# Four-layer kernel on 32 batches: layer 1's wide groups alternate between two PSUM banks

## What is computed

```python
def reference(x, t, itok, bias, dt, gate, mask, ...):
    # layer 0: conditioned block; LN is over the whole 256 x 256, scale and shift come from t
    h = silu(scale * LN(x) + shift) @ W_in + b_in
    x = silu(scale * LN(h) + shift) @ W_out + b_out + x
    # layer 1: attention, 16 heads of 16, bias 256 x 256 per head, keys masked by length
    x = LN(x) * (1 + s) + sh
    x = x + softmax(q k^T / 4 + bias, masked) v @ Wo + bo
    x = x + gelu_sigmoid((LN(x) * g2 + beta2) @ W1 + b1) @ W2 + b2      # 256 -> 1024 -> 256
    # layer 2: first and second differences of A*x and B*x on the 256 x 256 grid
    x = maximum(x + dt * df, 0)
    # layer 3: causal attention, then the same wide form with exact gelu, mixed by a gate
    y = x + softmax(causal(q k^T / 4)) v @ Wo + bo
    y = y + gelu(LN(y) @ W1 + b1) @ W2 + b2
    return x + gate * (y - x)
```

## Time and profile before

| | |
|---|---|
| three runs | 2603.47, 2604.91, 2608.86 us |
| median | 2604.91 us |
| the profiled execution | 2604.97 us, of which the span is 2603.7 us |
| TensorE busy | 2470.5 us (95%), 19148 matmuls |
| ScalarE busy | 2115.3 us (81%) |
| VectorE busy | 2043.6 us (78%) |
| GpSimd busy | 1536.1 us (59%) |
| mean granted TensorE clock | 0.984 of full |
| the two wide layers, groups (L1447, TN) | 3072 matmuls, 378.8 us busy, 38.7 us idle before them |

### The profile page before, as it was taken

How to read it: one execution, slowest core, us unless ns; L and a number is a source line. 1 busy time by engine, 2 the same in 40 slices (tenths; PEclk the granted TensorE clock), 3 DMA queues, 4 the chain that set the end, 5 groups by cost and what they waited for, 6 DMA issues and landing times.

```text
span 2603.7 us, 57961 instructions
## 1 busy us (share of the span) xinstructions
PE 2470.5 (95%) x19148; PEld 2005.6 (77%) x19148; DVE 2043.6 (78%) x7387; ACT 2115.3 (81%) x4694; POOL 1536.1 (59%) x1487
## 2 busy tenths in 40 slices
PE   6878999999999999999999999999999999999987
PEld 5666778778877877887887788778878877877776
DVE  6787878788888778888787888878888888878653
ACT  2466888888898888889888888988888888888875
POOL 2566666556666656666665656666556576655421
PEclk6899999999999999999999999999999999999999
DMA  5433443333344333334443333444433344433211
GB/s 205 120 119 105 121 127 113 111 106 106 107 122 126 112 110 108 107 105 122 126 115 108 108 107 106 122 127 115 114 110 100 105 121 125 123 105 96 75 29 33
DMA packets 178537, 287.67 MB, mean 110 GB/s; under 512 B 46080, under 2 KB 99328, under 8 KB 177984
## 3 DMA queue, kind: packets, MB, share of 16 engines
q1 hardware_dynamic: 178240, 283.97, 38.5%
HBM read 174.64 MB, written 8.45 MB: 70 GB/s over the span
## 4 chain that ended last, share of the span: by engine, by line
PE 69%; DVE 15%; SPq 4%; ACT 4%; issue 3%; POOL 2%; DMA 2%; DVEq 0%; POOLq 0%; ACTq 0%
PE bank L1525 17%; PE bank L1447 12%; PE bank L1548 10%; PE bank L1538 6%; PE bank L1563 6%; PE bank L1507 6%; DVE PB L1010 4%; PE bank L1514 3%; SPq L496 3%; PE bank L1459 3%; PE bank L1701 2%; DVE bank L969 2%; PE bank L1436 2%; SPq L492 1%; DMA Ks<-KU 1%
## 5 line engine op out<-in xcount | busy, mean ns | idle before, releaser
L1249 ACT ACTIVATE PB<-PB,mx 128x256 f32<-128x256 f32 (+1 forms) x2048 | 831.4, 473 | 35.7 <-DVE mx L1010 34.7
L579 POOL TENSOR_TENSOR BT<-BT,MN 128x1024 f32<-128x1024 f32 x256 | 556.9, 2180 | 122.5 <-DMA BT<-in_bias 121.0
L1548 PE MATMUL bank<-ident,PB 128*128 128x128 f32 x3584 | 486.4, 274 | 11.5 <-ACT PT L1254 5.5
L1010 DVE CUSTOM_DVE_ANT_0 PB<-bank,BT 128x256 f32<-128x256 f32 x1024 | 372.0, 418 | 137.8 <-PE bank L1538 132.8
L1548 PEld LDWEIGHTS bank<-ident,PB 128*128 128x128 f32 x3584 | 421.6, 141 | 63.4 <-ACT PB L1249 10.6
L1447 PE MATMUL bank<-TN,WS_w 128*128 128x256 f16 x3072 | 378.8, 273 | 38.7 <-ACT BB L1275 19.6
L1538 PE MATMUL bank<-Ks,Qs 96*128 96x512 f32 (+1 forms) x1024 | 364.6, 430 | 25.5 <-DMA Ks<-KU 12.0
L1017 DVE COPY PT<-bank 128x512 f32<-128x512 f32 (+1 forms) x512 | 315.9, 617 | 87.5 <-PE bank L1548 85.8
L1447 PEld LDWEIGHTS bank<-TN,WS_w 128*128 128x128 f16 x3072 | 282.5, 98 | 120.1 <-ACT BB L1275 35.4
L1254 ACT ACTIVATE PT<-bank 128x512 f32<-128x512 f32 (+1 forms) x512 | 272.3, 532 | 94.9 <-PE bank L1548 90.6
L1010 DVE CUSTOM_DVE_ANT_0 PB<-bank,caus 128x128 f32<-128x128 f32 (+1 forms) x1024 | 306.6, 350 | 42.3 <-PE bank L1538 42.2
(11 more groups left out here) (285 smaller groups left out, 4735.9 us busy)
## 6 DMA issues: line engine op xcount, KB each, us to landing
BT<-in_bias SPq DMA_DIRECT2D x256, 512.0 KB, 4.3
Qs<-QH SPq DMA_DIRECT2D x512, 64.0 KB, 2.4
Ks<-KH SPq DMA_DIRECT2D x1024, 32.0 KB, 2.0
Qs<-QU SPq DMA_DIRECT2D x256, 64.0 KB, 2.4
Ks<-KU SPq DMA_DIRECT2D x512, 32.0 KB, 2.0
XT<-in_xT SPq DMA_DIRECT2D x32, 256.0 KB, 2.8
X<-in_x SPq DMA_DIRECT2D x32, 256.0 KB, 2.9
AB<-ada_rows SPq DMA_DIRECT2D x32, 256.0 KB, 3.7
```

The source lines that it names most:

```text
L579: G.op.tensor_tensor(v2(BT[k % 4]), v2(BT[k % 4]), MN[:, :].unsqueeze(1).broadcast_to([128, 2, 512]), ALU.add).then_inc(g_bt, 1)
L1010: V.op.tensor_tensor_reduce(PB[(2 * D + q) % 6][:, h * 256:h * 256 + w], bS[q][:, h * w:h * w + w], plus, -1.0, 3.0e38, ALU.add, ALU.min, ...
L1249: S.op.activation(o, o, ACT.Exp, scale=-1.0, bias=mx[u.layer][:, c:c + 1]).then_inc(a_exp, 1)
L1548: last = T.op.transpose(bP[h][:, c * 128:c * 128 + 128], PB[(2 * u.D + q) % 6][:, h * 256 + k * 128:h * 256 + k * 128 + 128], ident[:, :])
```

## The change

Five things, in one edit.

1. `wide_bank`: for layer 1 in batches 2 to 29 odd groups go to bank 2, even ones stay in bank 1. Group g then waits for the evacuation of group g-2, and for what bank 2 held before: the last output of an earlier batch (`v_o`) and the keys of the next batch (`a_k1`).
2. `key_bank`: layer 1's keys of batches from 3 on go to bank 2. They no longer wait for the queries' evacuation, but for bank 2's readers; the values wait for the queries' evacuation and no longer for the keys'.
3. `t3`, which also uses bank 2, waits in addition for all of layer 1's wide evacuations of the next batch.
4. `P`, `OWN` and `SPLIT` get new ticks; most pieces move a little.
5. `WARM` loses `n1_ones_0`, `win_1`, `w1_0` (three products behind each of four groups), `n2_ones_2`, `n1_ones_3` and `v1_3`; `v3` goes from 10 to 15. In matmuls of the trace: 160 to 120.

```diff
@@ P (and so for OWN and SPLIT)
-    "t1_out": -24, "t1_lo": -21, "x1_bo": -18, "q1": -19, "q1_out": -17, "q1_lo": -27, "k1": -15,
...
+    "t1_out": -24, "t1_lo": -22, "x1_bo": 8, "q1": -18, "q1_out": -18, "q1_lo": -37, "k1": -14,
...
 WARM = {
-    "start": 24, "c1": 12, "n1_ones_0": 2, "v1": 9, "win_1": 5, "w1_0": 3, "n2_ones_2": 1, "n1_ones_3": 4,
-    "v1_3": 1, "v3": 10,
+    "start": 24, "c1": 12, "v1": 9, "v3": 15,
 }
...
+        def key_bank(layer, b):
+
+            return bT_ if layer == 1 and b > 2 else front_bank(layer, b)
...
             if b == NB - 1:
                 return ((bM, bF) if layer == 1 else (bF, bM))[g % 2]
-            return bM if layer == 1 else bT_
+            if layer == 1:
+                return (bM, bT_)[g % 2] if 1 < b < NB - 2 else bM
+            return bT_
...
-                        to_cols(U, front_bank(x, b), a, lambda m: scale_of("p3", 4) if x == 3 and n == "q" else 1.0,
+                        to_cols(U, key_bank(x, b) if n == "k" else front_bank(x, b), a, lambda m: scale_of("p3", 4) if x == 3 and n == "q" else 1.0,
...
                 for b in at(t, f"k{x}"):
-                    T.wait_ge(a_q[x], 3 * b + 2)
-                    linear(front_bank(x, b), "k", H).then_inc(p_k[x], 1)
+                    if x == 1 and b > 2:
+                        T.wait_ge(v_ws, made("w3") + 21)
+                        T.wait_ge(v_o, 2 * (b - 3))
+                        T.wait_ge(v_v[3], b - 2)
+                    else:
+                        T.wait_ge(a_q[x], 3 * b + 2)
+                    linear(key_bank(x, b), "k", H).then_inc(p_k[x], 1)
                     keep(f"k{x}", b)
                 for b in at(t, f"v{x}"):
-                    T.wait_ge(a_k[x], 3 * b + 2)
+                    T.wait_ge(a_q[x], 3 * b + 2)
+                    if x == 3 or b < 3:
+                        T.wait_ge(a_k[x], 3 * b + 2)
...
                 for b, g in steps(t, "w1", 4, 2):
                     T.wait_ge(v_ws, made("p3"))
                     T.wait_ge(v_t2, b + 1)
-                    if b < NB - 1 or g == 0:
+                    if b < 2 or b == NB - 2 or g == 0:
                         T.wait_ge(a_w1, 8 * b + 2 * g)
                     else:
-                        T.wait_ge(v_v[1], NB)
                         T.wait_ge(a_w1, 8 * b + 2 * g - 2)
+                        if b < NB - 1:
+                            T.wait_ge(v_ws, made("w3") + 21)
+                            T.wait_ge(v_o, 2 * (b - 2))
+                            T.wait_ge(a_k[1], 3 * (b + 2) - 1)
+                        else:
+                            T.wait_ge(v_v[1], NB)
...
                     T.wait_ge(v_ws, made("w3") + 21)
+                    if b > 0:
+                        T.wait_ge(a_w1, 8 * min(b + 2, NB - 2))
                     turn(front_bank(3, b), Y3[b % 2]).then_inc(p_t3, 1)
```

More of the change, by code:

```diff
@@ L56 @@
 P = {
-    "score0": -1, "score1": -1, "bias0": 0, "bias1": 0, "exp0": 1, "exp1": 2, "flip0": 8, "flip1": 8, "ev0": 7,
-    "ev1": 9, "pv": 14, "cx": 13, "ct": 17, "pvn": 17, "ld_bt": -12, "mask_add": -23, "stack": -8, "ld_x": -78,
-    "ld_xn": -37, "ld_ab": -36, "ld_mask": -117, "mask": -34, "n1_stats": -75, "n1_ones": -69, "n1_sum": -69,
[6 rows of a table removed]
-    "f1": 74, "s_pm": 63, "s_b": 67, "s_r": 75, "s_rp": 82, "s_re": 96, "s_ha": 81, "s_w": 97, "s_ab": 97,
-    "s_row": 98, "s_mm": 103, "s_f": 103, "ld_w1": -24, "ld_sten": -46, "ld_w3": -277, "coefs": -21,
+    "score0": -1, "score1": -1, "bias0": 0, "bias1": 0, "exp0": 2, "exp1": 2, "flip0": 8, "flip1": 8, "ev0": 7,
+    "ev1": 8, "pv": 14, "cx": 13, "ct": 16, "pvn": 16, "ld_bt": -12, "mask_add": -27, "stack": -8, "ld_x": -97,
+    "ld_xn": -37, "ld_ab": -51, "ld_mask": -96, "mask": -48, "n1_stats": -82, "n1_ones": -68, "n1_sum": -67,
[6 rows of a table added]
+    "f1": 72, "s_pm": 57, "s_b": 71, "s_r": 72, "s_rp": 82, "s_re": 96, "s_ha": 74, "s_w": 97, "s_ab": 97,
+    "s_row": 95, "s_mm": 102, "s_f": 101, "ld_w1": -24, "ld_sten": -46, "ld_w3": -277, "coefs": -21,
     "split_p1": -55, "split_p1_hi": -50, "split_p1_lo": -45, "split_w1": -8, "split_w1_hi": -4, "split_w1_lo": -2,
     "split_p3": 46, "split_p3_hi": 50, "split_p3_lo": 54, "split_w3": 82, "split_w3_hi": 88, "split_w3_lo": 92,
[4 rows of a table removed]
-    "out": 74, "st_out": 71,
[4 rows of a table added]
+    "out": 73, "st_out": 67,
 }
@@ L91 @@
     -2: {
[15 rows of a table removed]
[L107 to L108 removed]
[13 rows of a table added]
+        "m4_b": 325, "ld_x": -111, "ld_xn": -61, "ld_ab": -84, "ld_mask": -20, "ld_bt_1": -17, "stack_1": -10,
+        "s_row": 98, "stack_3": -55, "st_out": 787,
     },
     -1: {
[6 rows of a table removed]
[L117 removed]
[7 rows of a table removed]
[L125 to L127 removed]
[10 rows of a table removed]
[L138 removed]
[8 rows of a table removed]
[L147 to L148 removed]
[7 rows of a table removed]
[L156 removed]
[7 rows of a table removed]
[L164 removed]
[14 rows of a table added]
+        "y3": 489, "m4_rstd": 528, "m4_b": 628, "ld_mask": -163, "ld_x": -110, "ld_xn": -93, "ld_ab": -74,
+        "ld_bt_1": -20, "stack_1": -20, "s_row": 96, "stack_3": -46, "st_out": 990,
+    },
[10 rows of a table added]
+        "pvn_1": 21, "m1": 50, "t2_lo": 50, "f1": 76, "s_r": 79, "s_rp": 87, "s_re": 87, "s_w": 102, "s_ab": 102,
[7 rows of a table added]
+        "m4_b": 47, "scr": -333, "ld_mask": -276, "ld_sten": -223, "ld_ab": -156, "ld_w1": -211, "ld_w3": -39,
+        "ld_bt_1": 3, "stack_1": 5, "s_row": 109, "stack_3": -3, "st_out": 80,
+    },
[15 rows of a table added]
+        "ld_mask": -19, "ld_ab": -35, "ld_bt_1": -1, "stack_1": 2, "s_row": 104, "stack_3": -15, "st_out": 71,
     },
@@ L168 @@
 SPLIT = {
-    "bias1_3": 1, "exp0_3": 2, "exp1_3": 3, "ev0_3": 8, "ev1_3": 10, "pv_3": 13, "cx_3": 12, "ct_3": 16,
-    "pvn_3": 18, "stack_3": -9,
+    "exp0_3": 1, "exp1_3": 3, "flip0_3": 7, "ev0_3": 8, "ev1_3": 9, "ct_3": 17, "pvn_3": 17, "stack_3": -16,
 }
```

9 lines of the change are left out of this document (removed), and 135 rows, old and new, of tables (OWN, P).

## The result

The changed kernel is slower by a little: 2610.89 us (median of 20 runs, 2605.94 to 2615.95) against 2605.12 us for before (20 runs, 2600.05 to 2612.08). The ratio is 1.0019, 95% interval 1.0011 to 1.0027. The prediction was 2595, faster. The time lies inside the range of 2582 to 2612 and on the wrong side of no change.

The account below looks back on a forecast made before the run. TensorE's column work plus its waits was taken to bound the kernel. From 2604.97 us, 7.3 came off for 28 batches at -0.26 and 2.5 for idle-time products, clock and edges 0: 2595 us, range 2582 to 2612.

Parts of the forecast that it names:

- What bounds the kernel, and the steady part: From 500 to 2241 us: TensorE's column work plus its waits set the end; the change gives -0.26 us a batch.
- the waits between the groups: Layer 1's wide groups: alternating banks remove waits for the previous group's evacuation, -0.80 us a batch.
- The wait on TN: t2's new place: the first wide group waits for the turned t2 through ScalarE and VectorE, +0.60 us a batch.
- Layer 3's transposes: Layer 3's wide layer: the ET pair moved ahead covers the eight transposes' wait on the turned t4, -0.23 us a batch.
- The wait on BB: Layer 3's second wide group: its wait for BB's evacuation grows by the moved ET pair, +0.22 us a batch.
- t3's +0.07: Turning Y in bank 2: t3 now waits for all four evacuations, +0.07 us a batch, between 0 and 0.15.
- the keys' term: Layer 1's keys in bank 2: values no longer wait for the keys' evacuation, -0.12 us a batch.
- rival (a): Steady stretch: new tables also remove waits before scores and transposes, 0.42 us a batch, 12 us less, 2583; chance 0.16.
- Idle-time products: Trace matmuls from 160 to 120, mainly at 18.40, 169.45 and 202.64 us: -2.5 us together, between 0 and -3.5.
- Head and last batches: Outside the steady stretch, where tables change by up to a hundred ticks: taken as 0, 6 us allowed either way.
- (b): Steady part: waits only move, 0.26 us a batch more at neighbours cancels the gain, 2602.5 us; chance 0.24.
- (c): t3 stuck behind a late fourth evacuation on ScalarE: 1.0 us a batch lost, slower, 2621 us; chance 0.20.

Follow-up runs that it names:

- e9: The kernel of e7 with layer 1's keys back in bank 0 and the values again behind the keys' evacuation; 2606.70 us, ratio 1.0005.
- e1: The kernel before with the changed kernel's list of idle-time products and nothing else of the change; 2603.76 us, ratio 0.9995.
- e7: The changed kernel with two ticks of the first batch as before, s_pm 56 to 60 and s_re 87 to 97; 2605.99 us, ratio 1.0003.
- e2: The kernel before without the idle-time products w1_0 between the first batch's wide groups; 2603.45 us, ratio 0.9993.
- e11: The kernel before with two first-batch ticks as in the changed kernel, s_pm 60 to 56 and s_re 97 to 87; 2606.82 us, ratio 1.0007.
- e3: The changed kernel with the idle-time products w1_0 put back; 2614.66 us, ratio 1.0027.
- e4: The changed kernel with the whole old list of idle-time products; 2613.74 us, ratio 1.0032.
- e10: The kernel of e8 with layer 3's 43 ticks of the last batch as before the change; 2624.14 us, ratio 1.0067.
- e12: The kernel of e8 with some of GpSimd's ticks of batches 1 and 2 as before; 2606.76 us, ratio 1.0006.
- e13: The changed kernel with s_re alone back at 97 in the first batch; 2611.05 us, ratio 1.0012.
- e14: The changed kernel with s_pm alone back at 60 in the first batch; 2611.66 us, ratio 1.0013.
- e5: The change's two-bank code with the tables and idle-time products of before, but for five ticks that t3 needs; 2672.40 us, ratio 1.0261.
- e6: The changed kernel with its new tables, but the banks and their waits as before; 2681.45 us, ratio 1.0294.
- e8: The kernel of e7 with the first wide group two ticks later in batches 2 to 29, behind P·V; 2605.03 us, ratio 1.0000.

## Why the prediction was wrong

*What bounds the kernel, and the steady part*: right. The period was to fall to 75.4 or 75.5 and is 75.39. By its terms: the waits between the groups, -0.80, are gone whole, 7.25 - 6.38 = 0.87 by the starts. The wait on TN, +0.60, is 0.41 by the idle and 0.62 by the starts (2.07 less 1.45). Layer 3's transposes give the -0.23, but the ET pair moved behind them takes 0.11 more, so -0.12. The wait on BB, +0.22, is (18.7 - 13.7) / 23 = +0.22. t3's +0.07 is 0.72 - 0.66 = +0.06. The ET pair ahead of the values takes 0.22 us (1939.20 to 1939.42) instead of 0.34, the -0.12 of the keys' term, but it takes 0.22 in e9 too, with the keys back in bank 0: the size is right, and the order gives it, not the bank. That makes -0.21. A further -0.18 is the small waits of scores and transposes that are gone, which I had given to rival (a) and counted as 0. Together that is -0.39, and the starts of the batches give -0.35 for the forecast's -0.26: 8.0 us in 23 batches.

*Idle-time products*, -2.5 between 0 and -3.5: not decided. e1 gives a ratio of 0.9995, -1.3 us, with an interval that holds 0 and -2.5. My list of places also left out ten products at 81.7 us and two at 266.7, which have no term in the sum.

*Head and last batches*, 0 with plus or minus 6: **this is the step that failed.** The head measured +12.1, and the last batches +2.5, which the spread of executions covers. I had counted idle time that the new tables could give or take as a share of the idle of before, a sixth of 36.1 us, without following the order of GpSimd and VectorE in any of these batches. The order of the two engines at one place, which was there to be read, held 3.9 us of wait. e7 gives 4.9 us of time back by the medians (2605.99 against 2610.89) and some 4 by the ratios (1.0003 against 1.0019). The other 7 us or so of the head is not settled. At least 3 us of it lie between the first wide groups of batch 1 and batch 3: they are 140.9 to 143.0 us apart in the kernel before, e1, e2 and e11, and 146.3 to 148.5 in the changed kernel, e3, e4, e7 to e10 and e12 to e14. Of theories tried, the omitted products (e1 to e4) and GpSimd's loose pieces (e12) are out; the banks are out for the part up to batch 1 (e5, e6). The clock moves with the head in part: in 132 to 240 us it is 0.86 with batch 5 at 510.8 us, 0.89 at 505.6 (e7), 0.94 at 504.3 (e8), but 0.92 at 508.3 (e4). Whether the lower clock makes lateness or the waits make the lower clock, these runs don't separate.

*Rivals.* (a) came true in part, 0.18 of its 0.42 us a batch (above). (b), the waits only move, had called for 2602.5 and came out neither in the time nor in its mechanism: the steady part did gain. Its form is seen in e8, where the TN wait moved to t3. (c), t3 behind the fourth evacuation, had the right sign of the change by luck. It did not happen in the changed kernel, where the fourth evacuation ends ahead of t3; in e5 its two waits are 0.35 + 1.05 = 1.4 us of the 2.2 lost a batch, more than the 1.0 I had given it. The rule that double buffering PSUM "gave no further gain" (the Trainium skill, "TensorE: Matmul & The Clock Gate", section "HAM oscillation"), which I had lent to (b) and which the page reports of one kernel, does not carry over to this kernel: e6 against the changed kernel shows a gain of 2.4 us a batch from it in one order, and e5 a loss in the other.

The range was built around 0 for the head, and its upper end of 2612 holds the result only because 6 us for the edges and 3.4 for the clock had been put on rival (b). Its lower end of 2582 is (a)'s 2583 less 1, for no reason given. Nothing here is clearly faster than before. e8's profiled execution is the shortest of all, 2600.3 us, but its median is that of before.
